# Moving the softmax normalisation of grouped attention layers from VectorE to ScalarE and GpSimd

## What is computed

```python
xn = rmsnorm(x, norm_w)
q = (xn @ wq).reshape(B, T, N_HEADS, HEAD_DIM)
k = (cond @ wk).reshape(B, S, N_KV_HEADS, HEAD_DIM)
v = (cond @ wv).reshape(B, S, N_KV_HEADS, HEAD_DIM)
qg = q.reshape(B, T, N_KV_HEADS, n_rep, HEAD_DIM)
scores = jnp.einsum('btgrd,bsgd->bgrts', qg, k) * scale
attn = jax.nn.softmax(scores.astype(jnp.float32), axis=-1).astype(q.dtype)
out = jnp.einsum('bgrts,bsgd->btgrd', attn, v).reshape(B, T, N_HEADS * HEAD_DIM)
return residual + out @ wo
```

## Time and profile before

| what | us |
|---|---|
| median of three runs | 4410.58 (4406.17 to 4411.35) |
| the profiled execution | 4408.93 |
| its span | 4407.1 |
| PE busy | 4202.3 (95%) |
| DVE busy | 2600.0 (59%) |
| ACT busy | 2016.3 (46%) |
| POOL busy | 1837.8 (42%) |

### The profile page before, as it was taken

How to read it: one execution, slowest core, us unless ns; L and a number is a source line. 1 busy time by engine, 2 the same in 40 slices (tenths; PEclk the granted TensorE clock), 3 DMA queues, 4 the chain that set the end, 5 groups by cost and what they waited for, 6 DMA issues and landing times.

```text
span 4407.1 us, 62744 instructions
## 1 busy us (share of the span) xinstructions
PE 4202.3 (95%) x19566; PEld 2623.9 (60%) x19566; DVE 2600.0 (59%) x3585; ACT 2016.3 (46%) x2505; POOL 1837.8 (42%) x921
## 2 busy tenths in 40 slices
PE   9999999998999999999889999999999999999998
PEld 7888888884555555555545555544555544554555
DVE  3122200015556555655677777777777778777777
ACT  2111211113334333443355666566665666656665
POOL 0000000003445444544355656555655656656655
PEclk9999999998999999999989999999999999999999
DMA  5333522234445444544523223332233223322233
GB/s 186 129 129 134 163 86 82 91 95 129 120 126 131 123 113 121 133 122 119 139 62 95 69 75 88 89 99 72 78 87 95 69 84 95 88 85 76 81 92 102
DMA packets 320881, 457.03 MB, mean 104 GB/s; under 512 B 46168, under 2 KB 118872, under 8 KB 320824
## 3 DMA queue, kind: packets, MB, share of 16 engines
q1 hardware_dynamic: 320824, 456.27, 36.5%
HBM read 222.77 MB, written 102.77 MB: 74 GB/s over the span
## 4 chain that ended last, share of the span: by engine, by line
PE 34%; DVE 6%; ACT 5%; issue 5%; ACTq 0%; SPq 0%; DVEq 0%; POOL 0%; DMA 0%
PE a_ps L1202 7%; PE a_ps L1162 7%; PE a_ps L1227 6%; PE a_ps L1186 6%; PE a_ps L1144 5%; ACT a_probs L926 4%; DVE x_lo L1015 2%; PE a_ps L1213 1%; DVE a_max_cols L1009 1%; PE a_ps L1218 1%; DVE a_stage L1025 1%; PE a_ps L1169 1%; PE a_ps L1132 1%; DVE a_qf L999 0%; DVE a_results L1047 0%
## 5 line engine op out<-in xcount | busy, mean ns | idle before, releaser
L1009 DVE TENSOR_REDUCE a_max_cols<-a_ps 128x1 f32<-128x512 f32 x2086 | 1344.5, 678 | 301.2 <-PE a_ps L1162 297.3
L926 ACT ACTIVATE a_probs<-a_ps 128x1024 f32<-128x1024 f32 x1024 | 1016.5, 1026 | 693.5 <-PE a_ps L1186 690.6
L824 POOL TENSOR_TENSOR a_sums<-a_probs 128x1024 f32<-128x1024 f32 x256 | 606.9, 2387 | 771.4 <-ACT a_probs L926 771.4
L1162 PE MATMUL a_ps<-a_k_ops,a_q_ops 96*128 96x512 f32 x2086 | 860.7, 443 | 40.9 <-DVE a_qf L999 11.3
L1025 DVE RECIPROCAL a_stage<-a_stage 128x128 f32<-128x128 f32 x640 | 573.2, 925 | 462.6 <-ACT a_stage L907 462.6
L1186 PE MATMUL a_ps<-a_q_ops,a_k_ops 128*128 128x512 f32 x2560 | 789.4, 410 | 54.6 <-ACT a_probs L926 39.7
L824 POOL TENSOR_TENSOR a_sums<-a_sums,a_probs 128x1024 f32<-128x1024 f32 x320 | 765.7, 2405 | 20.7 <-POOL a_sums L824 20.0
L1162 PEld LDWEIGHTS a_ps<-a_k_ops,a_q_ops 96*128 96x128 f32 x2086 | 387.4, 190 | 532.1 <-DVE a_max_cols L1009 354.2
L1202 PE MATMUL a_ps<-a_probs,a_v 128*32 128x512 f32 (+1 forms) x4096 | 645.6, 606 | 33.4 <-ACT a_probs L926 31.9
L1186 PEld LDWEIGHTS a_ps<-a_q_ops,a_k_ops 128*128 128x128 f32 x2560 | 459.6, 190 | 283.6 <-ACT a_probs L926 180.1
L897 ACT ACTIVATE a_q_ops<-a_ps 1x512 fp32r<-1x512 f32 x518 | 305.1, 589 | 291.2 <-PE a_ps L1169 284.7
(11 more groups left out here) (87 smaller groups left out, 5236.8 us busy)
## 6 DMA issues: line engine op xcount, KB each, us to landing
a_k_ops<-k_scratch SPq DMA_DIRECT2D x201, 256.0 KB, 4.0
a_q_ops<-a_qn_hi SPq DMA_DIRECT2D x792, 64.0 KB, 2.0
k_scratch<-cp_out SPq DMA_DIRECT2D x88, 512.0 KB, 2.8
a_q_ops<-a_qn_hi SPq DMA_DIRECT2D x268, 128.0 KB, 2.3
cp_raw<-in_ctx_t SPq DMA_DIRECT2D x64, 512.0 KB, 4.0
x_raw<-out_t SPq DMA_DIRECT2D x26, 1024.0 KB, 5.5
a_q_ops<-a_qn_lo SPq DMA_DIRECT2D x396, 64.0 KB, 2.0
a_x_res<-out_t SPq DMA_DIRECT2D x96, 256.0 KB, 3.4
```

Source lines behind the costliest of these rows:

```text
L824: pool.tensor_tensor(sums[:, hp], (probs if i == 1 else sums)[:, hp], probs[:, n], ALU.add)\
L926: act.activation(probs[:, s], ps[:, 2 * (s % 2):2 * (s % 2) + 2, :], ACT.Exp)\
L1009: dve.tensor_reduce(max_cols[:, t % 2, col:col + 1], bank(max_bank(p)), AX.X, ALU.max, negate=True).then_inc(reduced, 1)
L1162: pe.matmul(bank(max_bank(p)), q_ops[0:SHIFT, s, h, PASS - 1, q * P:(q + 1) * P], k_ops[0:SHIFT, s, k_head(h), PASS - 1, :], start=True, s ...
```

## The change

It concerns the grouped layers only.

- ACT copies the sums of values out of PSUM into a new buffer `out_raw` (`take_outputs`), behind the shift and so ahead of the next tile's exponentials. PE's next sums of values wait for this copy, no longer for the normalising.
- POOL normalises: `out_raw` times the reciprocals in `stage`, behind the sums of the next tile.
- The four reciprocals of a tile stand behind the second, fourth, sixth and eighth maximum of the next tile; those of tile 3 in the closing block.
- ACT rounds the output of tile `t - 2` behind the first exponential of tile `t` (tiles 2 and 3), and POOL takes its rest ahead of the sums of tile `t`. Tiles 2 and 3 are rounded at the end.
- In the closing block PE projects tiles 0 and 1 for all four blocks first, then tile 2, then tile 3, and the four `add_result` come last. The first projection into bank 3 waits until the last denominators have been copied.

The core of the diff:

```diff
@@ gpsimd
+            def normalise(it, t):
+                pool.wait_ge(recip_done, (it * T + t + 1) * PARTS)
+                pool.wait_ge(out_taken, 1 + it * T + t + 1)
+                pool.tensor_tensor(stage[:, t % 2, :], out_raw[:, :], stage[:, t % 2, :], ALU.mult).then_inc(normed, 1)
                 for t in range(T):
+                    if has_norm and t > 1:
+                        rest_output(it, t - 2)
                     sum_probs(it, t)
-                    if t > 0:
+                    if not has_norm and t > 0:
+                        rest_output(it, t - 1)
+                    if has_norm and t > 0:
+                        normalise(it, t - 1)
+                    if has_norm and t == T - 1:
                         rest_output(it, t - 1)
                     rest_q(*place(it, t + AHEAD))
+                    if has_norm and t == T - 1:
+                        normalise(it, t)
                     if t == T - 1:
                         rest_output(it, t)
@@ scalar
+            def take_outputs(it, t):
+                act.wait_ge(pv, 1 + (it * T + t + 1) * KT)
+                act.wait_ge(normed, 1 + it * T + t)
+                act.activation(out_raw[:, :], bank(OUTB), ACT.Copy).then_inc(out_taken, 1)
-                        if t > 0 and s == NS // 2:
+                        if has_norm and t > 1 and s == 0:
+                            round_output(it, t - 2)
+                        if not has_norm and t > 0 and s == NS // 2:
                             round_output(it, t - 1)
                     shift(*place(it, t + 1))
+                    if has_norm:
+                        take_outputs(it, t)
+                    if has_norm and t == T - 1:
+                        round_output(it, t - 1)
@@ vector, grouped_tile and the closing block
                     reduce_max(it, p + i)
-                    if t > 0 and i == 0:
-                        normalise(it, t - 1)
+                    if t > 0 and i % 2 == 1 and i // 2 < PARTS:
+                        reciprocals(it, t - 1, range(i // 2, i // 2 + 1))
-                reciprocals(it, t, range(2))
...
-                    for i in range(5):
+                    for i in range(PARTS):
+                        reciprocals(it, T - 1, range(i, i + 1))
+                        reduce_max(it, FIRST[T] + 2 * i)
+                        reduce_max(it, FIRST[T] + 2 * i + 1)
+                    for i in range(8, 12):
                         reduce_max(it, FIRST[T] + i)
...
+                    for o in range(CK):
+                        add_result(it, o)
@@ tensor
-                    pe.wait_ge(normed, 1 + it * T + t)
+                    pe.wait_ge(out_taken if has_norm else normed, 1 + it * T + t)
+                if OB[o] == DENB and 0 in tiles and has_norm:
+                    pe.wait_ge(den_taken, 1 + (it + 1) * T)
+                    pe.wait_ge(o_lo, (it + 1) * T - 2)
+                    for o in range(CK):
+                        project_out(it, o, [0])
+                        maxima(it, p + 2 * o)
+                        project_out(it, o, [1])
+                        maxima(it, p + 2 * o + 1)
                     pe.wait_ge(o_lo, (it + 1) * T - 1)
...
+                    for o in range(CK):
+                        project_out(it, o, [2])
+                        maxima(it, p + 8 + o)
                     pe.wait_ge(o_lo, (it + 1) * T)
...
+                    for o in range(CK):
                         project_out(it, o, [3])
```

More of the change, by code:

```diff
@@ L520, in attention_layers @@
             w_raw = sb("w_raw", [P, 1, 4 * W], F32)
+            out_raw = sb("out_raw", [P, S], F32)
             qf = sb("qf", [P, S], F32)
@@ L580, in attention_layers @@
         normed = sem("normed")
+        out_taken = sem("out_taken")
         o_hi = sem("o_hi")
@@ L790, in _ @@
         def _(pool):
-            for credit in (scored, pv, normed, den_taken, *stored):
+            for credit in (scored, pv, normed, den_taken, out_taken, *stored):
                 pool.sem_inc(credit, 1)
@@ L1069, in grouped_tile @@
                         split_x(it + 1, 0)
-                reciprocals(it, t, range(2))
                 if t == 0:
                     reduce_max(it, p + main)
-                reciprocals(it, t, range(2, 3))
-                if t == 0:
                     reduce_max(it, p + main + 1)
                 take_q(*place(it, t + AHEAD))
-                reciprocals(it, t, range(3, PARTS))
             def head_tile(it, t):
@@ L1107, in _ @@
                         head_tile(it, t)
-                normalise(it, T - 1)
                 if has_norm:
-                    for i in range(5):
-                        reduce_max(it, FIRST[T] + i)
-                    add_result(it, 0)
-                    reduce_max(it, FIRST[T] + 5)
-                    add_result(it, 1)
-                    for i in range(6, 9):
-                        reduce_max(it, FIRST[T] + i)
-                    add_result(it, 2)
-                    for i in range(9, 12):
-                        reduce_max(it, FIRST[T] + i)
-                    add_result(it, 3)
+                    for i in range(PARTS):
[3 more added lines that the diff above has]
+                    for i in range(8, 12):
+                        reduce_max(it, FIRST[T] + i)
+                    for o in range(CK):
+                        add_result(it, o)
                 else:
+                    normalise(it, T - 1)
                     for o in range(CK):
@@ L1352, in _ @@
                     pe.wait_ge(w_split, WCH * (it // B + 1))
-                    pe.wait_ge(o_lo, (it + 1) * T - 1)
-                    project_out(it, 0, [0])
-                    maxima(it, p)
-                    project_out(it, 0, [1])
-                    maxima(it, p + 1)
-                    project_out(it, 0, [2])
-                    project_out(it, 1, [0])
-                    maxima(it, p + 2)
-                    project_out(it, 1, [1])
-                    maxima(it, p + 3)
-                    project_out(it, 1, [2])
-                    pe.wait_ge(o_lo, (it + 1) * T)
-                    project_out(it, 0, [3])
-                    maxima(it, p + 4)
-                    project_out(it, 1, [3])
-                    maxima(it, p + 5)
-                    for o in range(2, CK):
-                        project_out(it, o, [0])
-                        maxima(it, p + 3 * o)
-                        project_out(it, o, [1])
-                        maxima(it, p + 3 * o + 1)
-                        project_out(it, o, [2])
-                        maxima(it, p + 3 * o + 2)
+                    pe.wait_ge(o_lo, (it + 1) * T - 2)
[4 more added lines that the diff above has]
+                        maxima(it, p + 2 * o + 1)
+                    pe.wait_ge(o_lo, (it + 1) * T - 1)
+                    for o in range(CK):
+                        project_out(it, o, [2])
+                        maxima(it, p + 8 + o)
+                    pe.wait_ge(o_lo, (it + 1) * T)
+                    for o in range(CK):
                         project_out(it, o, [3])
```

## The result

The changed kernel takes 4475.92 us in the median of 4 executions (4468.95 to 4479.23), the kernel before 4408.38 beside it (4400.70 to 4411.35): a ratio of 1.0154 [1.0135, 1.0172]. It is slower, 10 us under the predicted 4486. The execution that was profiled is the fastest of the four, 4468.95 us with a span of 4467.2.

What follows compares the result with a forecast made beforehand. TensorE bounds the kernel, busy 85.11 of 88.71 us an iteration, with POOL's sums having little to spare. Adding 1.63 + 1.29 + 0.3 = 3.22 us, x 24 = 77 us, to 4408.9 gives 4486 us; range 4440 to 4520.

Steps and rivals of the forecast that it cites:

- Tile 2, 1.63 us: PE's denominators needing POOL's fourth sum start 1.63 us later: copy 0.35, rounding 0.52, rest 1.25, less 0.49 to spare.
- tile 3, 1.29 us: PE's denominators needing POOL's fourth sum start 1.29 us later: rounding 0.52, rest 1.25, less 0.48 to spare.
- the reserve: Time POOL's sums have to spare before PE's last denominators: 0.49 us in tile 2, 0.48 in tile 3.
- What would show it: Signs in tiles 2 and 3: denominators 0.05 to 0.1 us behind the fourth sum, sums 1.25 later, PE waits some 0.8.
- PE would itself be 0.87 and 0.52 late by the exponentials.: In tiles 2 and 3, the part of PE's delay from late exponentials; the rest appears as waiting before the denominators.
- The closing block, 0.3 us: In the closing output projections, PE waits 0.3 us, between 0 and 0.6, for the rest of tile 3.
- The reciprocals among the maxima, 0: On VectorE, 0.93 us each, taken to cost 0 since PE's work between maxima covers them; uncovered, up to 0.93 each.
- The sum, 3.22 us an iteration: Tile 2's 1.63, tile 3's 1.29 and the closing block's 0.3; over 24 iterations 77 us.
- x_lo, taken at 0: End of tile 1: VectorE's split of x mostly still wins its race with POOL; cost 0, bound 1.25 us.
- Rival A: Tile 1's end: the split loses to POOL's normalising, 0.9 us in 16 iterations, 4500 us (4507 at most); chance 0.13.
- B: Tiles 2 and 3: slack hides POOL's 1.25 us, only exponentials count; 1.7 us an iteration, 4450 us; chance 0.10.
- C: Weight loads' 236.3 us waiting for maxima are PE's time; not slower, 4400 us at the ceiling; chance 0.04.

Runs made afterwards that it cites:

- e8: e6 with VectorE's reciprocals put back at the end of their own tile, leaving ScalarE's copy and GpSimd's normalising of the change: 4403.79 us, 1.0003 of the kernel before.
- e4: Kernel before, with GpSimd's rest of the output in tile 1 waiting until VectorE's split of x is done: 4392.89 us, 0.9979 of the kernel before.
- e9: e1 with GpSimd's normalising of tile 0 also waiting for VectorE's split of x: 4433.21 us, 1.0070 of the kernel before.
- e6: e7 with a third buffer for denominators and outputs, rounding back behind the fifth exponential, rest behind the sums: 4416.07 us, 1.0021 of the kernel before.
- e1: Changed kernel with GpSimd's rest of the output of tiles 0 and 1 moved ahead of the rest of Q: 4447.67 us, 1.0105 of the kernel before.
- e5: e7 with VectorE's reciprocals put back behind their own tile's maxima: 4467.07 us, 1.0138 of the kernel before.
- e7: Changed kernel with GpSimd's normalising of tile 0 waiting until VectorE's split of x is done: 4465.26 us, 1.0135 of the kernel before.
- e2: Changed kernel with two extra GpSimd subtractions an iteration, in its idle time ahead of the rest of Q: 4493.85 us, 1.0204 of the kernel before.
- e3: Changed kernel with two extra GpSimd subtractions an iteration, between the output's rest and the sums of tiles 2 and 3: 4531.75 us, 1.0299 of the kernel before.

## Why the prediction was right, point by point

- **Tile 2, 1.63 us; tile 3, 1.29 us.** Measured 1.62 (21.07 - 19.45) and 1.29 (19.96 - 18.67). The terms were sized rightly one by one: the copy 0.37 (e8 against e4; predicted 0.35), the rounding 0.54 (e9 against e8, predicted 0.52; these two differ in the reciprocals' place too, and in tile 2 it is 0.51 against e6, which has the reciprocals where e9 has them), and what the rest adds to these, 0.71 and 0.74 (changed against e1; 1.25 less the reserve, 0.76 and 0.77). What would show it was there: `L1237` 0.09 us behind the fourth sum, the sums 1.25 behind the start of the output's rest. Only PE's own waits for the sums are 0.52, not 0.8.
- **"PE would itself be 0.87 and 0.52 late by the exponentials."** e1 and e9 measure just that, 0.91 and 0.55 over the kernel before and e4. My later expectation for e1, that the whole 1.25 us would be won back, forgot that sentence; the rival in it was the prediction's own.
- **The closing block, 0.3 us.** Measured 0.22, by the reciprocals and what follows them, as the chain in the prediction had it (e5).
- **The reciprocals among the maxima, 0.** True of the changed kernel (e5's 21.06 and 19.95 against e7's 21.07 and 19.95), but only under the cover of the late exponentials and sums. Without this cover they cost 0.33 us in tile 3 (e6 against e8). The prediction gave the cover a different name, PE's own work between maxima, and that one is not enough.
- **The sum, 3.22 us an iteration.** Measured 3.14 (91.87 - 88.73), 75 us instead of 77.
- **x_lo, taken at 0.** This is the term that was off most. From one profiled execution to the other the change costs 60 us, not 77. About 10 of the 17 us lie in the five iterations in which the kernel before had lost the split: there the two traces differ by 0.3 to 1.9 us instead of 3.14. Against e4, which loses none, these five cost 9.4 us by the traces, and the medians differ by 9.6. The changed kernel's execution lost none of 21, but e1, e2 and e3, with the same order around the split, lost 5, 9 and 11. So that it lost none is likely a draw and no property of the change; but 0 of 21 beside 25 of 63 would be a rare draw, and it isn't shown. Rival A was then a rival of every execution, not of the change as such. That the median came within 10 us of 4486 is in part luck: it depends on how many splits each execution lost.
- **Not priced at all:** the iterations that also load weights. The first of each layer lose 0.7 to 1.9 us rather than 3.1, since the reciprocals no longer stand behind the chunk and ahead of the taking of Q in tile 0; e5 gives part of this back. That takes 5 us off the sum, and 4 us more lie ahead of the loop's first tile 0, whose `L1237` comes that much earlier in the changed kernel (e5 against e7 puts 1.5 us of it on the reciprocals' place, the rest is open). The last of each layer lose 2.8 to 5.6 us, 3 us more together than the sum has; in tile 1 reciprocals, chunk and split follow one another on VectorE. Of two of these three, e7's wait takes back 1.8 and 3.0 us. The reciprocals' place is worth 0.2 to 1.5 us in them by e7 against e5, and 1.7 to 2.8 us by e6 against e8 (97.12 and 98.22 us against 95.43); I have not taken that further apart.
- **Rivals B and C.** B's world, in which GpSimd's 1.25 us are hidden, is that of e1 and e9: 1.68 us more an iteration (90.41 - 88.73), where B had 1.7. In the changed kernel they are not hidden. That e1's time, 4447.67, is close to B's 4450 us is luck, since five splits were lost in e1; without lost splits it is 4433 (e9). C fell by the list of waits: 236.3 us became 241.7.

## What to carry to other kernels

A reserve between two engines is worth more than a share of busy time: here 1.77 us of new work met half a microsecond of reserve in front of PE's queue, and that made nearly all of the 1.5%, while 4.4 us an iteration taken off an engine that nobody waited for won nothing. Moving work to a half-idle engine is free only where that engine stands idle anyway; ask for the place in its queue, not its load, and keep enough buffers that the moved work can stay out of the chain. Where two engines' operations exclude each other at one place in every iteration, let one wait for the other by a semaphore, rather than leave it to a race.

## What the runs showed of the hardware

**Who wins the pair of VectorE's split and a GpSimd operation isn't settled by who asks first.** In the changed kernel and in e1 to e3 the split starts, by the records, 0.17 to 0.22 us ahead of GpSimd's normalising (the 0.47 in the expectation of e7 was a misreading), and while GpSimd's last sum is still running; in the kernel before it is 0.82 to 0.88 us ahead of GpSimd's operation in 20 of 21 iterations, and lost 5. It went first in 21 of 21 iterations of the changed kernel, but in 16, 12 and 10 of e1, e2 and e3. One that was lost in e1, VectorE and GpSimd:

```profile
3188.12 3.64 DVE L1038 TENSOR_TENSOR x_lo<-x_raw,x_hi 128x2048 fp32r<-128x2048 f32 x1
```

```profile
3188.34 1.27 POOL L844 TENSOR_TENSOR a_stage<-a_out_raw,a_stage 128x512 f32<-128x512 f32 x1
```

If anything, the lost ones of e1 to e3 lie at the upper end (0.19 to 0.22 us ahead, the won ones of e3 0.19 to 0.21). 3.64 is 2.38 and the 1.26 that GpSimd's operation took. The Trainium skill (SBUF — State Buffer, section "SBUF: two separate sides") says that the engine that starts first holds the shared ports for its whole instruction. The trace agrees on the holding, 3.64 beside 1.27 us here and 2.37 beside 3.33 in the changed kernel. The use that rival A made of the rule, that the one who asks first wins, falls: in e1 to e3 the split had asked first and lost 25 of 63. What decides between two that both wait for GpSimd's sum to end, no run here shows.

**The same wait of PE is followed by full clock or by half.** After a lost split in e1, PE waits 1.82 us ahead of the projection of Q, here in two iterations:

```profile
2456.20 0.47 PE L1160 MATMUL a_ps<-x_hi,wq_hi 128*128 128x512 f32 x1 [1.82 <-DVE x_lo L1038]
...
3191.91 0.47 PE L1160 MATMUL a_ps<-x_hi,wq_hi 128*128 128x512 f32 x1 [1.82 <-DVE x_lo L1038]
```

In the first the projection then ran at a granted clock of 0.50, the lower of the two levels (1.2 GHz), in the second at 1.00, the upper. Two stretches of 2.80 us (us, busy PE and matmuls, PEld, DVE, ACT, POOL, clock, DMA):

```profile
2456.90:2459.70 2.80, 2.80 (x8) 2.21 (x7) 0.00 (x0) 1.86 (x2) 0.00 (x0) 0.50 0.00 0
3192.50:3195.30 2.80, 2.80 (x14) 2.33 (x13) 0.38 (x1) 1.95 (x3) 0.00 (x0) 1.00 0.00 0
```

Eight matmuls against fourteen. So a lost split costs 0.9 us in tile 2 (three times in e1) or 2.5 us (twice). Over the kernel before, e1 and e3, PE's wait behind a lost split is 1.82 or 1.83 us, and in 5 of 21 cases the projection behind it takes 4.3 to 4.6 us instead of 3.0; in e2, where the wait is 2.81 to 2.83 us, it does so in 7 of 9. The longer wait is followed by half clock more often, and what it costs in a given iteration can't be foretold from the wait alone.
